# Count blocks built up to 42 quads ahead of the messages, two batches of visits a step behind them, and smaller layer 0 units from block 28 on

## Chip, cores and metric

One NeuronCore of a Trainium2 chip. The metric is the device time of one execution in microseconds (us); the median of the runs is compared.

## What is computed

Two graph layers on the same graph of 6,250 nodes and 200,000 edges, sorted by destination, features of width 128 in float32:

```
layer 0:  m   = silu([x[src], x[dst], edge_attr] @ W1 + b1) @ W2 + b2
          agg = segment_sum(m, dst)
          x1  = LN(x + LN(x + mlp([x, agg])) )
layer 1:  agg = segment_sum(x1[src], dst) / max(degree, 1)
          out = LN(x1 + relu(relu([x1, agg] @ W1 + b1) @ W2 + b2))
```

Layer 1 needs x1 of every source node, so it can start only where layer 0 has finished a block of nodes.

## The kernel before, in words

Edges come in tiles of 128, four tiles are a quad, seven quads a group: 391 quads with edges (NQ), 392 in all (QUADS), 56 groups. Nodes come in 49 blocks of 128 (NB). The main loop has a step for every quad. All five engines run the same loop over steps s (functions `fast` of `sync`, `gpsimd`, `vector`, `tensor`, `scalar` in build_edges), each with its own instruction order, joined by semaphores that count.

**The messages.** GpSimd gathers the rows P_d[src] of a quad with four indirect DMAs (line 885), up to seven quads ahead: the gather of quad s waits until VectorE has added quad s - 7. TensorE makes `products` (lines 1169 and 1172), VectorE adds the gathered rows (`add`, line 961), ScalarE applies silu (line 1384), TensorE sums the messages into the nodes of the group (`sums`, lines 1206 and 1208). After the seventh quad VectorE adds the group's sums to the sums of all nodes (`add_sums`, line 969).

**The counts.** For layer 1 the kernel makes, per group, a 128 x 6272 matrix of how often each source node meets each destination of the group. For every quad VectorE writes one-hot tiles (`hots`, lines 946 and 948) from the keys (`make_keys`, once a group, lines 913 to 922), TensorE multiplies them (`count`, line 1186, with a carry at line 1192), ScalarE copies the result into the buffer `counts` (`copy_counts`, line 1328, and a carry at line 1333). There are two such buffers, one for even and one for odd groups. When a group is complete, ScalarE's queue stores its buffer to HBM in four parts (`store`, line 1354), one a step at steps 1 to 4 of the next group; at step 5 VectorE waits for the four parts and zeroes the buffer for the group after that (`clear`, line 929). In the kernel before, the count of a quad is made in the step before its messages.

**Layer 0 units.** When all sums of a stretch of nodes are final, a unit of four blocks (UB) runs the update MLP and both layer norms in small parts over nine steps (`unit_step`) and leaves x1 in two float16 halves (x1h). The blocks 46 to 48 can only come after the last quad, as a unit that starts at step 392.

**Visits.** A visit (d, lo, hi) applies the count matrix of group d to the blocks lo to hi of x1: the matrix comes back from HBM (`load_visits`, line 774, on SyncE's queue), TensorE does two matmuls a block (`visit`, line 1222), VectorE adds the 128 x 120 result to the sums of layer 1 (`add_visit`, line 978). Each such addition begins with a register load of the group's base column. `plan_visits` puts them by hand: one batch of at most 14 blocks (VB) a step, at most two visits in it before step 392 and four from there on; a visit may come only when the blocks are ready and the matrix is stored.

**The end.** After step 391 come the last unit (steps 392 to 401), the remaining visits (to step 430) and, as visits complete, 13 last units of layer 1 (`last_step`: matmuls at lines 1282 to 1294, VectorE at 1087 to 1103, ScalarE at 1433 to 1445, then the store of the output), put into the steps by `plan_last`.

Of the kernel before, what the change touches and what calls it, by code (L numbers as in the profile page):

```python
# [24 lines left out]
P = 128  # L25
# [25 lines left out]
UB, LAST_B = 4, 46  # L51
# [3 lines left out]
RL, RZ = 8, 3  # L55
NQ = -(-(-(-N_EDGES // P)) // QT)
# [15 lines left out]
def plan_units():  # L72

    units, lo = [], 0
    while lo < LAST_B:
        hi = min(lo + UB, LAST_B)
        units.append((lo, hi, -(-(P * hi + SLACK) // 112) * GQ + 1))
        lo = hi
    return units + [(LAST_B, NB, QUADS)]


def plan_visits(units):

    done, visits, s = [0] * GROUPS, [], 0
    while sum(done) < GROUPS * NB:
        ready = max([hi for lo, hi, s0 in units if s0 + U_LEN <= s], default=0)
        zeroed = max([hi for lo, hi, s0 in units if s0 + 1 <= s], default=0)
        left = VB
        for _ in range(2 if s < QUADS else 4):
            best = None  # L90
            for d in range(GROUPS):
                if s < (d + 1) * GQ + GQ + 2 or zeroed < NB and 112 * d + SLACK + GW > P * zeroed:
                    continue
                n = min(ready - done[d], left)
                if n >= (4 if s < QUADS - 2 * GQ else 1) and (best is None or n > best[0] and (ready < NB or n > 9)):
                    best = (n, d)
            if best:
                n, d = best
                visits.append((s, d, done[d], done[d] + n))
                done[d] += n  # L100
                left -= n
        s += 1
# [8 lines left out]
VISITS_AT = {s: [i for i, v in enumerate(VISITS) if v[0] == s] for s, d, lo, hi in VISITS}  # L111
UNIT_AT = {s0 + k: (u, k) for u, (lo, hi, s0) in enumerate(UNITS) for k in range(-4, U_LEN + 1)}
LAST_VISIT = [max(i for i, (s, d, b0, b1) in enumerate(VISITS) if 112 * d - SLACK < P * hi) for lo, hi in LAST_UNITS]
# [3 lines left out]
def plan_last():  # L117

    start, now = {}, 0
    for s in range(QUADS, QUADS + 20 * GQ):  # L120
        start[s] = now
        blocks = sum(VISITS[i][3] - VISITS[i][2] for i in VISITS_AT.get(s, ()))
        now += max(0.1 * blocks, 0.3 * len(VISITS_AT.get(s, ())), 1.5 if s <= QUADS + U_LEN else 0.7)
    steps, first = [], 0
    for w in range(len(LAST_UNITS)):
        first = max(first, start[VISITS[LAST_VISIT[w]][0] + 1] + 2)
# [10 lines left out]
def plan_slots():  # L137
# [3 lines left out]
    for b, s in enumerate(sorted(VISITS_AT)):  # L141
        r = b % RA
        if s >= QUADS + LEAD:
            r, late = late % RT, late + 1
        slot[s], before[s], used[r] = r, used.get(r), s
        at, parts = 0, []
        for i in VISITS_AT[s]:
# [7 lines left out]
        pieces[s] = parts  # L155
        count[r] += len(parts)
        landed[s] = 16 * count[r]
# [6 lines left out]
def plan_loads():  # L164

    at, last = {}, 0
    for s in sorted(VISITS_AT):
        last = max(last, s - (AHEAD if s >= QUADS + AHEAD + LEAD else LEAD), -1 if BEFORE[s] is None else BEFORE[s])
        at.setdefault(last, []).append(s)
# [6 lines left out]
def plan_banks():  # L176

    bank, freed, last = [], [], [None, None]
    for k, s in enumerate(sorted(VISITS_AT)):
        for j, i in enumerate(VISITS_AT[s]):  # L180
            bank.append((k % 2, j))
            freed.append(last[k % 2])
        last[k % 2] = VISITS_AT[s][-1]
# [6 lines left out]
def changes_of_sums():  # L190

    n, at = 0, {}
    for s in range(ENDQ):
# [3 lines left out]
        for i in VISITS_AT.get(s - 1, ()):  # L197
            n += 1
            at["visit", i] = n
        if UNIT_AT.get(s, (0, 0))[1] == 1:  # L200
            n += 1
            at["zero", UNIT_AT[s][0]] = n
    return at
# [429 lines left out]
def build_edges(nc, ctx, sem, sb, v):  # L633
# [42 lines left out]
    first_i = [v["first_i0"], sb("first_i1", [P, GT], I32)]  # L676
    nodeE = [sb(f"nodeE{k}", [KQ, QT * P], BF16) for k in range(2)]
# [33 lines left out]
    onehots = sem("onehots")  # L711
    keyed, far, near = sem("keyed"), sem("far"), sem("near")
# [31 lines left out]
    def sync(sp):  # L744
# [17 lines left out]
        def load_visits(s):  # L762

            r = SLOT[s]
            if BEFORE[s] is not None:
                sp.wait_ge(l1_mm, VISITS_AT[BEFORE[s]][-1] + 1)
# [4 lines left out]
            for d, m, lo, hi, at in PIECES[s]:  # L771
# [48 lines left out]
        def fast():  # L820
            load_q(0)
            load_ids(1)
            v["table_stored"](sp)
            for s in range(ENDQ):
                g, q = divmod(s, GQ)
                if q == 1 and 1 <= g < GROUPS - 1:
                    sp.wait_ge(sum_mm, g * GQ)
                    load_ids(g + 1)
                unit_loads(s)
# [70 lines left out]
    def vector(dve):  # L900
        v["settled"](dve)
        V = nc.vector

        def make_keys(g):

            k = g % 2
            if g > 0:
                dve.wait_ge(s_in[k], 16 * ((g + 1) // 2))
            dve.wait_ge(i_in[k], 32 * (g // 2 + 1))
            D3 = dst_i[k][:]  # L910
# [1174 lines left out]
```

## Time and profile before

| | |
|---|---|
| median of 3 runs | 2164.84 us (2163.88 to 2165.56) |
| the profiled execution | 2164.69 us |
| its span, first to last instruction | 2162.5 us |
| busy: TensorE matmul / VectorE / ScalarE / GpSimd | 90% / 77% / 66% / 71% |
| mean granted clock of TensorE | 0.935 of full speed |
| indirect gathers of the loop | 1535 |
| additions of visits (line 978) | 432 |

The 2.2 us between span and time lie outside the instructions. Busy shares are means over the whole span and say little here: the start, the loop of 391 steps (from about 60 us to about 2015 us) and the end have different limits, and a queue that issues DMAs counts only the issue as busy.

### The profile page before, as it was taken

What the parts mean: (1) busy time and instruction counts of PE and PEld (TensorE: products, weight loads), DVE (VectorE), ACT (ScalarE), POOL (GpSimd) and SP (SyncE); (2) the same over time, 40 slices, a digit from 0 to 9 for tenths busy, and PEclk for the clock granted to TensorE, in tenths of its full rate; (3) what the DMA queues carried; (4) which work ended last, traced back from release to release, by engine and by line L of the source; (5) the groups of instructions that cost most, each with busy time, mean ns of one, the idle gap of its engine ahead of it and who ended that gap; (6) DMA issues with size and microseconds to landing.
All of it is one profiled execution on the core that took longest, in us unless ns stands there. A gap on an engine that the chain in (4) does not pass through costs nothing.

```text
span 2162.5 us, 59764 instructions
## 1 busy us (share of the span) xinstructions
PE 1943.1 (90%) x19625; PEld 1742.2 (81%) x19625; DVE 1669.0 (77%) x5633; ACT 1431.0 (66%) x3734; POOL 1530.5 (71%) x1633
## 2 busy tenths in 40 slices
PE   7898888888898898999998998998999999999885
PEld 7887777777787787888887887987888898998764
DVE  8688877877787887787887787888887878877344
ACT  3677766676686776776776676766776776776214
POOL 7577777777777777777777777777777777776121
PEclk9989988998898998998998999999999999999998
DMA  8567667675776776777787787888787798887871
GB/s 283 145 211 220 194 193 206 185 221 173 225 221 215 193 240 202 226 227 233 214 259 218 214 258 238 254 243 247 233 266 232 228 285 245 258 290 249 280 249 50
DMA packets 301154, 487.81 MB, mean 226 GB/s; under 512 B 120202, under 2 KB 175244, under 8 KB 300840
## 3 DMA queue, kind: packets, MB, share of 16 engines
q10 hardware_dynamic: 94017, 245.03, 34.4%
q1 hardware_dynamic: 154823, 129.94, 20.4%
q0 software_dynamic: 52000, 108.96, 19.3%
q8 instruction: 160, 2.62, 0.5%
q14 instruction: 154, 1.26, 0.2%
HBM read 375.62 MB, written 108.13 MB: 224 GB/s over the span
## 4 chain that ended last, share of the span: by engine, by line
POOL 48%; issue 19%; PE 15%; DVE 8%; DMA 7%; ACT 2%; DVEq 1%; ACTq 0%; SPq 0%; POOLq 0%
POOL gath L885 48%; DMA gath<-P_d,src_i 6%; PE ps_l L1222 3%; PE ps_pre L1169 3%; PE ps_cnt L1186 3%; DVE edgeK L948 2%; PE ps_sum L1206 2%; DVE pre L961 1%; DVE edgeL L946 1%; DVE sumT L978 1%; DVEq L975 1%; PE ps_p L435 1%; DMA A_v<-A_d 1%; PE ps_pre L1172 1%; ACT counts L1328 1%
## 5 line engine op out<-in xcount | busy, mean ns | idle before, releaser
L885 POOL DMA_INDIRECT gath<-P_d,src_i x1535 | 1455.3, 948 | 486.4 <-issue 455.4
L948 DVE TENSOR_SCALAR edgeK<-iotaK,key 128x500 bf16<-128x500 f16 (+1 forms) x1564 | 666.7, 486 | 0.0
L1169 PE MATMUL ps_pre<-wc,eT_c 128*128 128x128 f32 x3128 | 619.7, 320 | 2.4 <-issue 2.4
L1186 PE MATMUL ps_cnt<-edgeK,edgeL 128*128 128x250 bf16 (+1 forms) x3128 | 485.8, 304 | 78.9 <-ACT counts L1328 41.4
L1169 PEld LDWEIGHTS ps_pre<-wc,eT_c 128*128 128x128 f32 x3128 | 514.0, 206 | 25.3 <-issue 2.6
L1328 ACT ACTIVATE counts<-ps_cnt 128x1000 bf16<-128x1000 f32 x391 | 404.4, 1034 | 172.4 <-issue 90.5
L1206 PE MATMUL ps_sum<-edgeN,h 128*128 128x40 f32 x3128 | 428.1, 288 | 75.0 <-ACT h L1384 74.5
L1206 PEld LDWEIGHTS ps_sum<-edgeN,h 128*128 128x128 f32 x3128 | 398.3, 199 | 100.1 <-ACT h L1384 87.5
L961 DVE TENSOR_TENSOR pre<-ps_pre,gath 128x512 f32<-128x512 f32 x384 | 260.8, 679 | 266.7 <-DMA gath<-P_d,src_i 215.8
L1384 ACT ACTIVATE h<-pre 128x512 f32<-128x512 f32 x391 | 243.8, 624 | 264.3 <-DVE pre L961 262.7
L1186 PEld LDWEIGHTS ps_cnt<-edgeK,edgeL 128*128 128x128 bf16 x3128 | 290.9, 102 | 149.2 <-DVE edgeK L948 68.3
L1364 ACT ACTIVATE farN<-iotaN,rel_g 128x40 f32<-128x40 f16 x1564 | 381.1, 314 | 33.0 <-issue 31.0
L1172 PE MATMUL ps_pre<-Qw,nodeE 120*128 120x128 bf16 x1564 | 359.5, 230 | 0.0
L946 DVE TENSOR_SCALAR edgeL<-iotaL,low 128x132 bf16<-128x132 f16 x1564 | 327.2, 269 | 0.0
L1222 PE MATMUL ps_l<-A_v,x1h 128*128 128x120 bf16 x4856 | 295.3, 218 | 10.5 <-DMA A_v<-A_d 5.5
L1222 PEld LDWEIGHTS ps_l<-A_v,x1h 128*128 128x128 f16 x4856 | 271.9, 99 | 18.0 <-issue 8.1
L978 DVE TENSOR_TENSOR sumT<-ps_l,sumT 128x120 f32 x432 | 119.5, 277 | 101.0 <-PE ps_l L1222 47.5
L1172 PEld LDWEIGHTS ps_pre<-Qw,nodeE 120*128 120x128 bf16 x1564 | 164.4, 105 | 0.0
L1374 ACT ACTIVATE edgeN<-farN 128x160 f32<-128x160 f32 x391 | 125.9, 322 | 26.5 <-PE ps_sum L1208 26.2
L938 DVE TENSOR_SCALAR nodeE<-rel_c,pidq 120x512 bf16<-120x512 bf16 x391 | 141.2, 361 | 0.0
L1375 ACT ACTIVATE edgeB<-farN 128x160 bf16<-128x160 f32 x391 | 125.1, 320 | 0.0
L1333 ACT ACTIVATE carry<-counts 128x50 bf16 x335 | 96.6, 288 | 40.2 <-ACT counts L1328 0.8
(185 smaller groups left out, 1391.6 us busy)
## 6 DMA issues: line engine op xcount, KB each, us to landing
eT_c<-eT ACTq DMA_DIRECT2D x193, 512.0 KB
A_d<-counts ACTq DMA_DIRECT2D x168, 384.0 KB
rel_c<-rel_d ACTq DMA_DIRECT2D x193, 240.0 KB
A_v<-A_d SPq DMA_DIRECT2D x70, 448.0 KB
A_v<-A_d SPq DMA_DIRECT2D x111, 256.0 KB
gath<-P_d,src_i POOLq DMA_INDIRECT x1535
A_d<-counts ACTq DMA_DIRECT2D x56, 416.0 KB
Qw<-Q_d SPq DMA_DIRECT2D x56, 180.0 KB
```

Of the source, the lines that this page charges most:

```text
L885: pool.indirect_dma_start(gath[:, q, t * D:(t + 1) * D], None, v["P_d"], bass.IndirectOffsetOnAxis(ap=src_i[g % 2][:, c:c + 1], axis=0)).t ...
L946: V.tensor_scalar(edgeL[x][:, j, :], iotaL[:, :, 0:LC], low[k][:, q * QT + j:q * QT + j + 1], None, ALU.is_equal)
L948: last = V.tensor_scalar(edgeK[x][:, ROFF[j]:ROFF[j] + A2 * w], iotaK[j][:, :, 0:A2 * w // KR], key[k][:, q * QT + j:q * QT + j + 1], None ...
L961: V.tensor_tensor(pre[s % 2][:], ps_pre[s % 2][:], gath[:, q, :], ALU.add).then_inc(pre_add, 1)
L1169: T.matmul(o, eT_c[c % RE][:, e0:e0 + P], wc[:], start=True, stop=False)
L1172: last = T.matmul(o, nodeE[x][:, t * P:(t + 1) * P], Qw[g % 2][:, q, :], start=False, stop=True)
L1186: last = T.matmul(o[:, :, w0:w0 + w], edgeL[x][:, j, 0:P], r, start=(j == 0), stop=(j == QT - 1 and q == 0), skip_group_check=True)
L1206: T.matmul(ps_sum[:, cols], h[x][:, t, :], edgeN[x][:, t, :], start=False, stop=True, skip_group_check=True)
L1222: last = T.matmul(l1_part(i), x1h[:, a, part, :], A[:, (a - lo) * P:(a - lo) * P + GW], start=(a == lo and part == 0), stop=(a == hi - 1 a ...
L1328: A.activation(counts[k][:].rearrange("p (b a) d -> p b a d", b=2)[:, :, :, bass.ds(off, W0)], ps_cnt[:, :, 0:AB * W0].rearrange("p b (a d ...
L1364: last = A.activation(farN[:, j, :], iotaN[:, q, :, 0:WN // KR], ACT.Square, scale=-1.0, bias=rel_g[k][:, q * QT + j:q * QT + j + 1])
L1384: A.activation(h[x][:, :, 0:D], pre[x][:].rearrange("p (t n) -> p t n", n=D), ACT.Silu).then_inc(silu, 1)
```

## The change

- **Counts ahead.** `plan_counts` separates the step of a count from that of its quad. Until step 11 nothing changes. From step 12 to step 258, every sixth step makes a second ("extra") count, 42 in all, so that the counts run up to 43 quads ahead; the last count is made in step 347 instead of 390. Every extra count happens to be the seventh quad of a group. The stores of a group follow its copies, the clearing of a buffer follows the seventh one-hots of a group (now directly behind `hots`), and the keys of the next group are made behind its fourth.
- **Own index tiles.** The keys of group g + 1 are made from `src_c`, `dst_c`, `first_c`, loaded by three more small DMAs a group on SyncE's queue; the relative destinations of the messages are still made from the old tiles, in the new function `relate`.
- **Two batches a step.** Steps 357 to 391 have no count; they may have two batches of visits each, one ahead of `sums` and one behind, with up to three visits a batch. VectorE adds the first late in the same step and the second early in the next. `add_visits` reads all base columns of a batch before its first addition.
- **The ring of matrix buffers** grows from 4 to 12 slots at step 357 instead of 396, loads run 10 steps ahead from step 367 instead of 406.
- **Units of two blocks** from block 28 on: 17 units instead of 13.

What the planners give by this (blocks times groups, 2744 in all):

| | before | after |
|---|---|---|
| visits | 432 | 528 |
| block visits before step 392 | 2206 | 2392 |
| block visits from step 392 on | 538 | 352 |
| visits from step 392 on | 93 | 68 |
| of these in steps 392 to 404 | 15 | 12 |
| last step with a visit | 430 | 419 |
| last units with their VectorE part before the last visits | 8 | 3 |

The core of the diff:

```diff
-UB, LAST_B = 4, 46
+UB, LAST_B, FINE = 4, 46, 28
+EARLY, EVERY, FIRST_EXTRA = 42, 6, 12
...
-        hi = min(lo + UB, LAST_B)
+        hi = min(lo + (UB if lo < FINE else 2), LAST_B)
...
+def plan_counts():
+    main, extra, c, s = {}, {}, 1, 0
+    while c < NQ:
+        if s >= FIRST_EXTRA and s % EVERY == 0 and c - s - 1 < EARLY:
+            extra[s], c = c, c + 1
+        if c < NQ:
+            main[s], c = c, c + 1
+        s += 1
+    copied = {0: 0, **{c: s + 1 for s, c in main.items()}, **{c: s for s, c in extra.items()}}
+    stores = {}
+    for c in range(GQ, NQ):
+        if 1 <= c % GQ <= len(PARTS):
+            stores.setdefault(copied[c], []).append((c // GQ - 1, c % GQ - 1))
...
# plan_visits: t = 2 * step + (0 or 1)
+        s, second = divmod(t, 2)
+        if second and not COUNTED + LEAD <= s < QUADS:
+            t += 1
+            continue
-        for _ in range(2 if s < QUADS else 4):
+        for _ in range(2 if s < COUNTED + LEAD else 3 if s < QUADS else 4):
...
# vector
-        def add_visit(i):
-            base = dve.value_load(gbase[0:1, VISITS[i][1]:VISITS[i][1] + 1], min_val=0, max_val=NP_ - 1)
+        def add_visits(t):
+            made = VISITS_AT[t]
+            bases = [dve.value_load(gbase[0:1, VISITS[i][1]:VISITS[i][1] + 1], min_val=0, max_val=NP_ - 1) for i in made]
+            for i, base in zip(made, bases):
+                dve.wait_ge(l1_mm, made[-1] + 1)
+                dve.wait_ge(changed, CHANGE["visit", i] - 1)
+                V.tensor_tensor(sumT[:, bass.ds(base, GW)], l1_part(i), sumT[:, bass.ds(base, GW)],
+                                ALU.add).then_inc(changed, 1)
...
-                if s + 1 < NQ:
-                    if q == GQ - 1:
-                        dve.wait_ge(prepared, g + 2)
-                    hots(s + 1)
-                for i in VISITS_AT.get(s - 1, ()):
-                    add_visit(i)
+                for c in (COUNT_AT.get(s), EXTRA_AT.get(s + 1)):
+                    if c is not None:
+                        if c % GQ == 0:
+                            dve.wait_ge(prepared, c // GQ + 1)
+                        hots(c)
+                        if c % GQ == 3 and c // GQ + 1 < GROUPS:
+                            make_keys(c // GQ + 1)
+                        if c % GQ == GQ - 1:
+                            clear(c // GQ + 1)
+                for t in ADDED_EARLY.get(s, ()):
+                    add_visits(t)
                 unit_step(s)
                 split_biases(s)
                 if g + 1 < GROUPS and q == 2:
-                    make_keys(g + 1)
-                if g + 1 < GROUPS and q == 5:
-                    clear(g + 1)
+                    relate(g + 1)
...
+                if s in ADDED_LATE:
+                    add_visits(ADDED_LATE[s])
...
# tensor
-                for i in VISITS_AT.get(s, ()):
+                for i in VISITS_AT.get(2 * s, ()):
                     visit(i)
...
+                if s in EXTRA_AT:
+                    count(EXTRA_AT[s])
                 if s < NQ:
                     sums(s)
-                if s + 1 < NQ:
-                    count(s + 1)
+                for i in VISITS_AT.get(2 * s + 1, ()):
+                    visit(i)
+                if s in COUNT_AT:
+                    count(COUNT_AT[s])
...
# scalar
             for s in range(ENDQ):
+                made = 0 if s == 0 else COUNT_AT.get(s - 1)
+                if s + 1 < NQ:
+                    distances(s + 1)
+                if s in EXTRA_AT:
+                    copy_next(made)
                 if s < NQ:
                     activate(s)
                     load_chunk_of(s)
...
+                if s in EXTRA_AT:
+                    copy_next(EXTRA_AT[s])
+                elif made is not None:
+                    copy_next(made)
+                for g, part in STORES_AT.get(s, ()):
+                    store(g, part)
```

## Rows read from the trace of the kernel before

**Rows 1.** Page: chain that ended last, by engine; groups: line, op, xcount | busy, mean | idle.
```profile
POOL 48%; issue 19%; PE 15%; DVE 8%; DMA 7%; ACT 2%; DVEq 1%; ACTq 0%; SPq 0%; POOLq 0%
L885 POOL DMA_INDIRECT gath<-P_d,src_i x1535 | 1455.3, 948 | 486.4 <-issue 455.4
```

**Rows 2.** Line 885 and line 961, windows from 0 to 120 and 0 to 1300 us: count, min/median/max ns.
```profile
L885 POOL DMA_INDIRECT gath<-P_d,src_i x40: 938/944/1062, 69.4 to 119.9; - x40
L961 DVE TENSOR_TENSOR pre<-ps_pre,gath x5: 669/672/691, 102.4 to 117.1; 128x512 f32<-128x512 f32 x5
...
L885 POOL DMA_INDIRECT gath<-P_d,src_i x981: 938/944/1511, 69.4 to 1299.1; - x197
L961 DVE TENSOR_TENSOR pre<-ps_pre,gath x244: 619/690/693, 102.4 to 1297.7; 128x512 f32<-128x512 f32 x122
```

**Rows 3.** Busy time by stretch: PE, PEld, DVE, ACT, POOL, clock, DMA share, GB/s.
```profile
1920.00:1970.00 50.00, 50.00 (x634) 47.53 (x632) 40.84 (x147) 39.47 (x98) 37.81 (x41) 1.00 0.85 267
```

**Rows 4.** Timeline at the loop's end: start, duration, engine, line; in brackets idle before.
```profile
1993.03 0.94 POOL L885 DMA_INDIRECT gath<-P_d,src_i  x1 [0.30 <-issue]
...
2007.84 1.63 PE L1222 MATMUL ps_l<-A_v,x1h 128*128 128x120 bf16 x28
2009.31 1.04 PE L1206 MATMUL ps_sum<-edgeN,h 128*128 128x40 f32 x8
...
2008.04 0.69 DVE L961 TENSOR_TENSOR pre<-ps_pre,gath 128x512 f32<-128x512 f32 x1 [1.10 <-PE ps_pre L1172]
2014.74 0.29 DVE L969 TENSOR_TENSOR sumT<-ps_sum,sumT 128x128 f32 x1 [0.54 <-DVE sumT L978]
```

**Rows 5.** Waits of VectorE, windows 110:1370, then 900:1350: us, times, longest.
```profile
DVE pre L961 <- DMA gath<-P_d,src_i: 166.8, 75, 7.0
...
DVE pre L961 <- DMA gath<-P_d,src_i: 44.0, 22, 5.5
...
DVE counts L929 <- DMA A_d<-counts: 9.1, 4, 4.7
```

**Rows 6.** Timelines: VectorE's step and ScalarE's store; a store and the clearing it releases.
```profile
1136.81 0.68 DVE L961 TENSOR_TENSOR pre<-ps_pre,gath 128x512 f32<-128x512 f32 x1
1137.67 0.84 DVE L946 TENSOR_SCALAR edgeL<-iotaL,low 128x132 bf16<-128x132 f16 x4
1139.64 0.33 ACTq L1354 DMA_DIRECT2D A_d<-counts  x1
1140.05 0.27 DVE L978 TENSOR_TENSOR sumT<-ps_l,sumT 128x120 f32 x1
1141.51 0.69 DVE L961 TENSOR_TENSOR pre<-ps_pre,gath 128x512 f32<-128x512 f32 x1 [0.70 <-DMA gath<-P_d,src_i]
1145.87 0.33 ACTq L1354 DMA_DIRECT2D A_d<-counts  x1
...
1265.86 0.34 ACTq L1354 DMA_DIRECT2D A_d<-counts  x1
1270.77 0.72 DVE L929 MEMSET counts<- 128x800 uint32 x1 [1.81 <-DMA A_d<-counts]
```

**Rows 7.** Timeline of TensorE: the sums of a quad behind an idle stretch.
```profile
690.53 1.93 PE L1206 MATMUL ps_sum<-edgeN,h 128*128 128x40 f32 x8 [4.50 <-ACT h L1384]
```

**Rows 8.** Timelines of the end: a TensorE wait; VectorE's additions and last units.
```profile
2033.13 7.68 PE L1222 MATMUL ps_l<-A_v,x1h 128*128 128x120 bf16 x112 [4.60 <-DMA A_v<-A_d]
...
2051.79 0.28 DVE L978 TENSOR_TENSOR sumT<-ps_l,sumT 128x120 f32 x1 [2.87 <-PE ps_l L1222]
2052.61 0.28 DVE L978 TENSOR_TENSOR sumT<-ps_l,sumT 128x120 f32 x1 [0.54 <-PE ps_l L1222]
...
2135.80 0.68 DVE L1087 SCALAR_TENSOR_TENSOR eT_c<-ps_cnt,eT_c 128x512 f32<-128x512 f32 x1
2138.85 0.69 DVE L1087 SCALAR_TENSOR_TENSOR eT_c<-ps_cnt,eT_c 128x512 f32<-128x512 f32 x1 [0.79 <-PE ps_cnt L1294]
2142.63 0.69 DVE L1087 SCALAR_TENSOR_TENSOR eT_c<-ps_cnt,eT_c 128x512 f32<-128x512 f32 x1 [1.51 <-PE ps_cnt L1294]
```

More of the change, by code:

```diff
@@ L121, in plan_last @@
         start[s] = now
-        blocks = sum(VISITS[i][3] - VISITS[i][2] for i in VISITS_AT.get(s, ()))
-        now += max(0.1 * blocks, 0.3 * len(VISITS_AT.get(s, ())), 1.5 if s <= QUADS + U_LEN else 0.7)
+        blocks = sum(VISITS[i][3] - VISITS[i][2] for i in VISITS_AT.get(2 * s, ()))
+        now += max(0.1 * blocks, 0.3 * len(VISITS_AT.get(2 * s, ())), 1.5 if s <= QUADS + U_LEN else 0.7)
     steps, first = [], 0
     for w in range(len(LAST_UNITS)):
-        first = max(first, start[VISITS[LAST_VISIT[w]][0] + 1] + 2)
+        first = max(first, start[VISITS[LAST_VISIT[w]][0] // 2 + 1] + 2)
         steps += [(next(s for s in start if start[s] >= first + t), first + t, w, k) for k, t in enumerate(L_STEPS)]
@@ L140, in plan_slots @@
     count = [0] * RT
-    for b, s in enumerate(sorted(VISITS_AT)):
+    for b, t in enumerate(sorted(VISITS_AT)):
         r = b % RA
-        if s >= QUADS + LEAD:
+        if t // 2 >= COUNTED + LEAD:
             r, late = late % RT, late + 1
-        slot[s], before[s], used[r] = r, used.get(r), s
+        slot[t], before[t], used[r] = r, used.get(r), t
         at, parts = 0, []
-        for i in VISITS_AT[s]:
+        for i in VISITS_AT[t]:
             _, d, lo, hi = VISITS[i]
@@ L166, in plan_loads @@
     at, last = {}, 0
-    for s in sorted(VISITS_AT):
-        last = max(last, s - (AHEAD if s >= QUADS + AHEAD + LEAD else LEAD), -1 if BEFORE[s] is None else BEFORE[s])
-        at.setdefault(last, []).append(s)
+    for t in sorted(VISITS_AT):
+        s = t // 2
+        last = max(last, s - (AHEAD if s >= COUNTED + AHEAD + LEAD else LEAD), -1 if BEFORE[t] is None else BEFORE[t] // 2)
+        at.setdefault(last, []).append(t)
     return at
@@ L202, in changes_of_sums @@
             at["zero", UNIT_AT[s][0]] = n
+        for i in VISITS_AT[ADDED_LATE[s]] if s in ADDED_LATE else ():
+            n += 1
+            at["visit", i] = n
     return at
@@ L676, in build_edges @@
     first_i = [v["first_i0"], sb("first_i1", [P, GT], I32)]
+    src_c, dst_c, first_c = ([sb(f"{n}_c{k}", [P, GT], I32) for k in range(2)] for n in ("src", "dst", "first"))
     nodeE = [sb(f"nodeE{k}", [KQ, QT * P], BF16) for k in range(2)]
@@ L711, in build_edges @@
     onehots = sem("onehots")
+    related = sem("related")
+    c_in = [sem(f"c_in{k}") for k in range(2)]
     keyed, far, near = sem("keyed"), sem("far"), sem("near")
@@ L828, in fast @@
                     load_ids(g + 1)
+                for c in range(GQ + 1, NQ, GQ):
+                    if COUNT_STEP[c] == s and c // GQ + 1 < GROUPS:
+                        load_count_ids(c // GQ + 1)
                 unit_loads(s)
@@ L1106, in fast @@
         def fast():
+            relate(0)
             make_keys(0)
@@ L1451, in fast, with copy_next @@
         def fast():
-            off = 0
+            offset = [0]
+            def copy_next(c):
+                ahead = 0
+                if c % GQ < GQ - 1 and c + 1 < NQ:
+                    ahead = act.value_load(offs[0:1, c + 1:c + 2], min_val=0, max_val=LASTQ)
+                copy_counts(c, offset[0], ahead)
+                offset[0] = ahead
             distances(0)
```

100 lines of the change are left out of this document (53 added, 47 removed).

## The prediction, made before the kernel was run

> **What bounds the kernel now.** I read the page's chain first, then the groups of instructions, the stretches, and timelines of one step and of the end. In the chain GpSimd has 48% and nearly all of it is line 885 [rows 1]; the gathers take 0.948 us and are followed by 0.30 us of their own issue (455.4 us in 1494 gaps), so one comes every 1.25 us and a quad every 4.98 us. The reader is to see that GpSimd waits for nobody: 1535 gathers at that pace are 1915 us, and they run from 69.4 [rows 2] to 1993.03 [rows 4]. The loop cannot be shorter than that whatever the other engines do. Counting gathers / 4 less additions gives how far GpSimd leads VectorE beyond the seven quads of the start: 5.0 quads at 120 us, 1.25 at 1300 us [rows 2]. It may lead by 7. So 5.75 quads, 28.6 us, of lateness can be absorbed before a gather is held up.
>
> Late in the loop this changes: from 1920 to 1970 us TensorE is busy for 50.00 of 50 us at full clock [rows 3], because every step there has a full batch of 14 blocks, and the last gathers wait to be used. The quad of the last gather (1993.03) is added at 2008.04, and the last sums are in at 2014.74 [rows 4]. From there to the end of the span (2162.5) are 147.8 us. That tail is in three stretches. (1) 2014.74 to 2051.79: the last unit and 15 visits, with a wait of 4.60 us for a matrix. (2) 2051.79 to 2135.80: 78 visits, whose additions come 0.82 us apart in a chain on VectorE (0.28 us, then 0.54 us idle), with VectorE's part of 8 last units among them [rows 8]. 78 x 0.82 = 64, so the 8 units take the other 20, 2.5 us each. (3) 2135.80, the ninth last unit, to the end: 26.7 us; consecutive units are 3.78 us apart (2138.85, 2142.63) [rows 8].
>
> **The change, part by part.**
>
> *The counts leave the end of the loop.* After step 347 a step has no one-hots (2.38 us of VectorE: from 1137.67 to 1140.05 [rows 6]), no count on TensorE and no copy on ScalarE. TensorE is then no longer full at the end, and the addition of quad 390 follows its gather. The gather lands when VectorE could first use it: with the least lead seen, about 1 quad or 4 to 5 us behind the issue at 1993.03, at 1998.7. Then addition 0.69, silu and sums (1.04 us for their first part [rows 4]) need about 2.8 us: last sums at 2001.5 instead of 2014.74, if no gather was held up. Against it stand the six additions a step of steps 362 to 372 and 378 to 388. At 0.82 us each they are 4.9 us, more than the room; with the base columns read first, and under other work, 0.48 us each, 2.9 us, beside about 0.9 us for the rest. The bounds of a step are thus 3.8 and 5.8 us against 4.98, for some 22 steps: no lateness, or 18 us. I take 2 us.
>
> *The extra counts.* 42 of them, every sixth step (29.9 us of gathers). Each adds 2.38 us to VectorE. More: all are seventh quads, so `clear` now comes directly behind their one-hots, and the fourth part of the store it waits for is issued in the same step instead of the one before. From the addition the store is issued 2.83 us later (1136.81, 1139.64) or 4.36 (1141.51, 1145.87), and it takes 4.91 us to land (1265.86, 1270.77). VectorE reaches `clear` 3.24 us (1136.81 to 1140.05) plus 2.38 us behind the addition [rows 6]. So it waits between 2.1 and 3.65 us each time; I take 3.0. Queued behind it are this step's additions of visits and the next quad's addition, for which ScalarE and TensorE wait. Together 5.4 us per six steps. Against that stands the idle time which VectorE had: for gathers 166.8 us from 110 to 1370, of which 44.0 from 900 to 1350, and 9.1 us there for the same clearings [rows 5]. Per six steps that is 2.9 + 0.6 = 3.5 us late, and early (166.8 - 44.0) / 790 x 29.9 = 4.6 plus 0.7 for the lead won back, 5.3. Early the account is even. Late, 15 periods (steps 168 to 258, where most visits are) are short by 1.9 us each, 29 us: just the 28.6 us of lead. TensorE idles in each long step and then runs slowly: the sums behind 4.50 us of idle took 1.93 us [rows 7] against 1.04 [rows 4], which is the lower of the clock's two levels, 1.2 instead of 2.4 GHz. With the count as much again, at most 1.8 us each time, 27 us over 15 periods if all of it lay on the path and none if it lies beside VectorE's work; I take 8 us of held gathers.
>
> The Trainium skill ("DMA: Bandwidth & Descriptors", section on the anatomy of one DMA) has a fit for one DMA issued from GpSimd, 2.0 us plus the bytes at 436 GB/s. For a part of 384 KB that would be an estimate of 2.9 us where the trace shows 4.91 for a store from ScalarE's queue; the wait would then be 0.1 to 1.6 us instead of 2.1 to 3.65, and no gather would be held. The trace has the duration for the very transfer, so the sum goes by 4.91.
>
> *The tail.* Stretch 1: three visits and one batch of step 392 go (1.47 us on TensorE, 2007.84 to 2009.31 [rows 4], and 3 x 0.82 on VectorE), as does the matrix wait of 4.60, since loads now run ten steps ahead; with smaller waits behind it 11 us, 37 to 26. Bounds: 5 us (the unit's own chain of small steps sets it) and 13. Stretch 2: 56 visits instead of 78, 46 us, and 3 units at 2.6 among them instead of 8: 54 instead of 84. TensorE's 174 fewer blocks of this stretch (0.105 us each) lie beside this. Stretch 3: five more units at 3.78 before the last four: 26.7 + 18.9 = 46 us. Sum 126 instead of 147.8.
>
> *Costs beside other work.* Four more units between steps 246 and 380, in a stretch where ScalarE is busy for 39.47 of 50 us and VectorE for 40.84 [rows 3]; without that cover each would cost about what stretch 1 of the end takes without its visits, 37.1 - 15 x 1.47 = 15 us. Three more index DMAs a group stand on SyncE's queue, asked for two steps before their keys; if the queue were stuck behind a matrix load for more than two steps, the keys and all behind them would wait. `relate` moves one small subtraction. I cost them at nothing.
>
> *Sum.* 2001.5 + 8 + 2 = 2011.5, plus 126 is a span of 2137.5; with the 2.2 us around the span 2139.7. The profiled execution was 2164.69, the median 2164.84, so no correction: 2140 us, 1.1% less.
>
> **The rivals.**
>
> *The clearings don't bite.* VectorE's idle time takes them in and no gather is held: 2001.5 + 126 + 2.2, about 2130, or 2122 with the better bounds of the tail. For it: the waits for gathers are 166.8 us. Against it: they are not where the visits are.
>
> *The extra counts hold the gathers (slower).* Place: steps 12 to 258, VectorE in `clear`, GpSimd at line 885 for the addition of seven quads before. With 3.65 us of waiting and 1.8 us of cold clock each period costs 7.8 us: short by 2.5 in 27 periods and 4.3 in 15, 132 less 28.6 of lead, 103 us; 2001.5 + 103 + 126 + 2.2 = 2233. It decides against the change from a shortage of about 60 us, that is from 6.0 us a period on in place of 5.4 and something. Mild forms end between 2165 and 2190.
>
> *The late additions or the unit chain take back the gain.* Six additions a step at 0.82 give 16 us more than assumed, or the last unit's chain gives only 5 of 11: together 2160; one of them 2146 to 2156.
>
> *The change makes the counts early but the tail is not set by visits:* the 13 last units at 3.78 us are 49 us by themselves; were they to start no earlier than now, the tail would lose only stretch 1: 2150.
>
> **How the numbers follow.** My forecast has 0.42, clearings that don't bite 0.20, held gathers 0.20 (slower, nearly all), late additions or chain 0.12, unmoved tail 0.06. Two in a thousand of this kernel (4.3 us) is about what a measurement can tell from no change. Faster: all but the held gathers and a part of the late additions, 0.76; within 0.2%: 0.05; slower: 0.19. The range goes from 2122 (nothing held, best tail) to 2172 (the mild part of the slower case); the dear end of that case stays outside.
>
> **What the profile would show.** Gathers / 4 less additions at 1300 us: between 5 and 7 quads (forecast), under 3 (clearings don't bite), 7 from 600 us on, and waits of line 885 for line 961 (slower). Waits at line 929 of 2 to 4 us in about 42 places, some 120 us in all. Last gather near 2001, last sums near 2011, visits over 80 us behind that, and 56 additions in the last 54 of these. Wrong it would be above all if the gathers end after 2030, or if the clearings wait for under 1 us.

## The result and the profile after

The changed kernel takes 2361.93 us (median of 4 runs, 2356.34 to 2365.39) against 2164.61 for the kernel before: a ratio of 1.0913, 95% interval 1.0899 to 1.0926, or 197 us slower. The forecast was 2140 and 1.1% faster. The profiled execution has a span of 2358.9 us, 196.4 more than before, and everything below is told against spans. Four kernels were first run on a chip where the granted clock was 0.80 to 0.82, the kernel before took 2964.11 us, before_first 2982.91, extra_third 3055.43, both_units4 3057.73 and both_two 3057.86, and were run again elsewhere; only the later runs (labels ending in _b) are used, so nothing below is shown for such a chip.

The page of the kernel after, chain and groups (columns as in [rows 1]):

```profile
PE 38%; DVE 32%; issue 16%; DVEq 6%; ACT 5%; DMA 2%; ACTq 1%; SPq 0%; POOL 0%; POOLq 0%
...
L937 POOL DMA_INDIRECT gath<-P_d,src_i x1535 | 1455.6, 948 | 659.3 <-issue 440.4
L985 DVE MEMSET counts<- 128x800 uint32 (+1 forms) x56 | 42.6, 761 | 236.0 <-DMA A_d<-counts 235.7
```

GpSimd had 48% of the chain [rows 1] and has none of it now. The gathers are as many and as long as before, but the idle time ahead of them grew from 486.4 to 659.3 us. The second row is new among the costly groups: clearing a count buffer is 42.6 us of work with 236.0 us of idle VectorE ahead of it. The list of waits (engine, line, what it waited for: us, times, longest) says what was behind both:

```profile
DVE counts L985 <- DMA A_d<-counts: 235.7, 54, 8.2
POOL gath L937 <- DVE pre L1017: 99.7, 62, 12.3
POOL gath L937 <- DMA src_i<-src_pt: 99.2, 24, 10.9
```

In the kernel before, the same list had (line 929 is its clearing, line 961 its addition of gathers):

```profile
DVE pre L961 <- DMA gath<-P_d,src_i: 215.8, 110, 7.0
DVE counts L929 <- DMA A_d<-counts: 37.5, 18, 5.1
```

The waits for arriving gathers, which were VectorE's idle time before, are gone altogether. GpSimd now waits for VectorE (its lead of seven quads is used up), and at the turn of a group also for its own index tile, which SyncE loads only in the group before.

One clearing in full, from the timeline of the kernel after (answers to [rows 6] and [rows 7]):

```profile
993.22 0.69 DVE L1017 TENSOR_TENSOR pre<-ps_pre,gath 128x512 f32<-128x512 f32 x1 [0.96 <-PE ps_pre L1236]
994.84 1.71 DVE L1004 TENSOR_SCALAR edgeK<-iotaK,key 128x500 bf16<-128x500 f16 x4
998.57 1.71 DVE L1004 TENSOR_SCALAR edgeK<-iotaK,key 128x500 bf16<-128x500 f16 x4
999.75 0.33 ACTq L1422 DMA_DIRECT2D A_d<-counts  x1
1005.28 0.72 DVE L985 MEMSET counts<- 128x800 uint32 x1 [5.00 <-DMA A_d<-counts]
1008.65 0.66 DVE L1017 TENSOR_TENSOR pre<-ps_pre,gath 128x512 f32<-128x512 f32 x1
1009.34 0.63 ACT L1450 ACTIVATE h<-pre 128x512 f32<-128x512 f32 x1 [5.29 <-DVE pre L1017]
1009.58 0.94 POOL L937 DMA_INDIRECT gath<-P_d,src_i  x1 [8.29 <-DVE pre L1017]
1012.01 2.10 PE L1250 MATMUL ps_cnt<-edgeK,edgeL 128*128 128x250 bf16 x8 [0.80 <-DVE edgeK L1004]
```

VectorE writes the one-hots of two quads (line 1004 twice), is at the clearing at 1000.28 and stands there for 5.00 us, because ScalarE issued the fourth part of the store only at 999.75 and it landed 5.53 us later. The next quad's addition comes 15.4 us behind the one before it. ScalarE waited 5.29 us for it and GpSimd 8.29. The next count took TensorE 2.10 us. The Trainium skill ("PSUM — Partial Sum Buffer", section on engine and sequencer instructions) says that the queues of ScalarE, VectorE and GpSimd are strictly first in, first out; the trace agrees: the addition that GpSimd needed stood behind a clearing with which it has nothing to do.

Busy time by stretch in the kernel after (columns as in [rows 3]):

```profile
400.00:900.00 500.00, 429.72 (x3815) 377.08 (x3814) 392.01 (x1340) 335.26 (x865) 342.65 (x361) 0.88 0.66 197
900.00:1370.00 470.00, 399.30 (x3859) 354.19 (x3858) 359.63 (x1229) 302.46 (x777) 314.32 (x332) 0.90 0.69 206
1820.00:2100.00 280.00, 255.50 (x2921) 237.19 (x2921) 174.52 (x574) 165.57 (x456) 202.76 (x215) 0.94 0.86 259
```

No engine is full in any of them: VectorE is busy for 77 to 78% of the first two stretches and nevertheless sets the pace. Of the 108.0 and 110.4 us in which it is idle there, 71.7 and 71.1 are the wait at line 985. The granted clock of TensorE is 0.88 to 0.90 there.

The end of the loop and the end of the kernel (timelines; they answer to [rows 4] and [rows 8]):

```profile
2166.52 0.94 POOL L937 DMA_INDIRECT gath<-P_d,src_i  x1 [0.30 <-issue]
2208.80 0.29 DVE L1025 TENSOR_TENSOR sumT<-ps_sum,sumT 128x128 f32 x1 [2.55 <-PE ps_sum L1272]
...
2242.59 0.28 DVE L1036 TENSOR_TENSOR sumT<-ps_l,sumT 128x120 f32 x1 [0.21 <-DVE sumT L1036]
...
2243.55 0.28 DVE L1036 TENSOR_TENSOR sumT<-ps_l,sumT 128x120 f32 x1 [0.20 <-DVE sumT L1036]
2246.24 0.28 DVE L1036 TENSOR_TENSOR sumT<-ps_l,sumT 128x120 f32 x1 [2.40 <-PE ps_l L1286]
```

The 196.4 us lie in three places. The last gather is at 2166.52 instead of 1993.03 (173.5). The last sums follow it by 42.3 us instead of 21.7 (20.6). From there to the end of the span are 150.1 us instead of 147.8 (2.3). In the tail four additions come 0.48 us apart (0.28 and 0.20 idle), then 2.41 us of nothing: 2.2 us more than between two additions, so about 0.55 for each of the four reads of base columns. A batch of four takes 4.14 us (2242.10 to 2246.24), where single reads gave 4 x 0.82 = 3.28 [rows 8].

### The profile page after: what moved, and what is told of

It is laid out like the page before. It is cut to its first block, busy times and chain, and to the rows that moved or that the text cites. A ratio compares the mean times of both kernels' runs of the same rounds, so it can differ in the third digit from the quotient of the medians.

```text
span 2358.9 us, 60784 instructions
## 1 busy us (share of the span) xinstructions
PE 2020.4 (86%) x19657; PEld 1803.8 (76%) x19657; DVE 1706.5 (72%) x5757; ACT 1457.9 (62%) x3770; POOL 1530.9 (65%) x1633
## 4 chain that ended last, share of the span: by engine, by line
PE 38%; DVE 32%; issue 16%; DVEq 6%; ACT 5%; DMA 2%; ACTq 1%; SPq 0%; POOL 0%; POOLq 0%
DVE edgeK L1004 13%; PE ps_pre L1233 9%; PE ps_cnt L1250 9%; PE ps_l L1286 7%; PE ps_sum L1270 6%; DVE edgeL L1002 6%; DVEq L1032 4%; DVE pre L1017 3%; DVE sumT L1036 3%; DVE nodeE L994 2%; PE ps_pre L1236 2%; ACT counts L1396 2%; DMA first_i<-dst_first 1%; ACT h L1450 1%; DMA A_v<-A_d 1%
## 5 line engine op out<-in xcount | busy, mean ns | idle before, releaser
L937 POOL DMA_INDIRECT gath<-P_d,src_i x1535 | 1455.6, 948 | 659.3 <-issue 440.4
L1233 PE MATMUL ps_pre<-wc,eT_c 128*128 128x128 f32 x3128 | 627.8, 323 | 2.6 <-issue 2.6
L1250 PE MATMUL ps_cnt<-edgeK,edgeL 128*128 128x250 bf16 (+1 forms) x3128 | 501.1, 310 | 64.1 <-ACT counts L1396 40.7
L1233 PEld LDWEIGHTS ps_pre<-wc,eT_c 128*128 128x128 f32 x3128 | 523.6, 210 | 28.9 <-issue 2.7
L1270 PE MATMUL ps_sum<-edgeN,h 128*128 128x40 f32 x3128 | 442.9, 294 | 100.0 <-ACT h L1450 99.4
L1270 PEld LDWEIGHTS ps_sum<-edgeN,h 128*128 128x128 f32 x3128 | 412.0, 205 | 120.6 <-ACT h L1450 108.2
L1250 PEld LDWEIGHTS ps_cnt<-edgeK,edgeL 128*128 128x128 bf16 x3128 | 299.1, 104 | 143.1 <-issue 43.6
L1286 PE MATMUL ps_l<-A_v,x1h 128*128 128x120 bf16 x4320 | 275.0, 222 | 82.4 <-DVE sumT L1036 80.0
L1286 PEld LDWEIGHTS ps_l<-A_v,x1h 128*128 128x128 f16 x4320 | 250.6, 101 | 92.5 <-issue 86.4
L1036 DVE TENSOR_TENSOR sumT<-ps_l,sumT 128x120 f32 x528 | 147.6, 280 | 227.5 <-PE ps_l L1286 116.1
L985 DVE MEMSET counts<- 128x800 uint32 (+1 forms) x56 | 42.6, 761 | 236.0 <-DMA A_d<-counts 235.7
```

The costliest lines, as they stand in the source:

```text
L937: pool.indirect_dma_start(gath[:, q, t * D:(t + 1) * D], None, v["P_d"], bass.IndirectOffsetOnAxis(ap=src_i[g % 2][:, c:c + 1], axis=0)).t ...
L1233: T.matmul(o, eT_c[c % RE][:, e0:e0 + P], wc[:], start=True, stop=False)
L1250: last = T.matmul(o[:, :, w0:w0 + w], edgeL[x][:, j, 0:P], r, start=(j == 0), stop=(j == QT - 1 and q == 0), skip_group_check=True)
L1270: T.matmul(ps_sum[:, cols], h[x][:, t, :], edgeN[x][:, t, :], start=False, stop=True, skip_group_check=True)
L1286: last = T.matmul(l1_part(i), x1h[:, a, part, :], A[:, (a - lo) * P:(a - lo) * P + GW], start=(a == lo and part == 0), stop=(a == hi - 1 a ...
```

## The experiments

My theory after reading this profile: two faults add up. The clearing now stands right behind the one-hots of a quad whose step also brings the last store (the greater part, in the loop), and the reads of all base columns ahead of a batch lengthen each batch by about 0.2 us an addition (at the loop's end and in the tail). The rivals: the 42 extra counts and the additional visits are themselves too much for VectorE; or the index tiles of the gathers, for which GpSimd waits 99.2 us, come too late by themselves.

### The clearing later, the bases singly, both, and no extra counts

**clear_later** puts the clearing behind the one-hots of the next group's first quad.

```diff
-                        if c % GQ == 0:
-                            dve.wait_ge(prepared, c // GQ + 1)
                         hots(c)
+                        if c % GQ == 0:
+                            clear(c // GQ)
...
-                        if c % GQ == GQ - 1:
-                            clear(c // GQ + 1)
```

> The changed kernel (2361.9 us) with the clearing of a count buffer moved one step later: behind the one-hots of the first quad of the next group, not of the seventh quad. Counts, visits and all costs stay. Theory A (the clearings hold VectorE, its lateness holds the gathers): the clearing waits fall from 235.7 us to under 90, the last gather comes before 2080 instead of 2166.5, the time is 2250 to 2290. Rival B (the extra one-hots and counts are too much by themselves, wherever the clearing stands): the clearing waits fall but the last gather stays beyond 2130 and the time beyond 2320. Rival C (the index tiles of the gathers come late, 99 us of waits at the gather line): these waits stay near 99 us and hold the time beyond 2300.

Measured: 2221.06 us (the kernel before took 2166.66 on that chip), span 2219.2. This and the next three kernels, and the four with _b, were executed once each; how far single executions of one kernel can lie apart is seen at both_again. Two waits from the list of waits:

```profile
DVE counts L985 <- DMA A_d<-counts: 44.1, 28, 4.1
POOL gath L937 <- DMA src_i<-src_pt: 30.8, 8, 7.4
```

The clearing's wait fell from 235.7 to 44.1 us and the time by 140.9 us, more than I had expected. The wait for the index tile fell with it, from 99.2 to 30.8, and is 6.6 in the kernel with both edits: it followed the lateness and was no cause of its own. All of the gain is in the loop: the last gather is at 2026.7 (139.8 us earlier), while the last sums still follow it by 42.4 us and the tail is still 150.1 us.

**base_each** reads each base column right before its own addition, as in the kernel before.

```diff
-            bases = [dve.value_load(gbase[0:1, VISITS[i][1]:VISITS[i][1] + 1], min_val=0, max_val=NP_ - 1) for i in made]
-            for i, base in zip(made, bases):
+            for i in made:
+                base = dve.value_load(gbase[0:1, VISITS[i][1]:VISITS[i][1] + 1], min_val=0, max_val=NP_ - 1)
```

> The changed kernel with each base column read right before its own addition of a visit, as in the kernel before, instead of all of a batch first. Theory (a read costs the sequencer some 0.55 us and is hidden under an addition only if it stands between two): a batch of four visits in the end takes 3.3 us instead of 4.14, the 15 batches there 12 us less, the steps with six visits about 1 us less each; the time is 2325 to 2345. Rival (reading first hides the reads, as I had forecast): 2362 to 2385.

Measured: 2319.31 us, 42.6 less than the changed kernel and a little beyond the range. The last gather comes 14.4 us earlier (2152.1), the last sums follow it by 25.6 us instead of 42.3, and the tail is 139.8 us instead of 150.1. The clearing still waits 241.4 us. Each edit moves mainly its own parts of the time: the lag of the last sums and the tail move with the reads, the waits of the clearing with its place.

**both** has both edits.

> Both edits together: clearing one step later, base columns read one by one. If the two causes are separate, the gains add: 2215 to 2270. If the lateness at the clearings only uncovers another limit (index tiles, late steps), less than the sum: beyond 2280.

Measured: 2165.32 us, 196.6 below the changed kernel and 50 below my range. That is 13 us more than the sum of the two alone (140.9 + 42.6 = 183.5), but this kernel scatters by more than that, as the rounds below show, so whether the two help each other stays open. The page and waits of this kernel:

```profile
PE 30%; DVE 21%; POOL 20%; issue 13%; ACT 6%; DMA 4%; DVEq 3%; ACTq 2%; SPq 0%; POOLq 0%
...
L937 POOL DMA_INDIRECT gath<-P_d,src_i x1535 | 1454.8, 948 | 491.7 <-issue 456.1
...
DVE pre L1017 <- DMA gath<-P_d,src_i: 46.8, 24, 7.4
DVE counts L985 <- DMA A_d<-counts: 42.1, 25, 4.2
```

The gathers run freely again, to 1998.0. VectorE has 46.8 us of waiting for gathers left of 215.8 in the kernel before. In rounds (**both_again**) this kernel took 2168.07 us (2157.42 to 2184.81), a ratio of 1.0015 with an interval of 0.9986 to 1.0044: level with the kernel before, and 193.9 us below the changed kernel. Its profiled execution, the third slowest of ten, has the last gather at 2004.8 and the last sums at 2034.7, where that of both has 1998.0 and 2023.7: differences of that size between single executions show nothing.

> The same kernel as in both, timed in rounds: 2162 to 2169 us, not to be told from the kernel before.

**no_extra** keeps everything of the change but makes no count ahead (`EARLY` 0 instead of 42).

> The changed kernel without any extra count: each count in the step before its quad, so clearings stand as in the kernel before; own index tiles, the reading of base columns first and units of two blocks stay; the planner then leaves 456 block visits and 77 visits for step 392 on and no step has two batches. Theory A: the last gather comes within 10 us of 1993 and the time is 2165 to 2195. Rival D (the new index tiles or the finer units hold the loop): the last gather comes after 2030 and the time is over 2210.

Measured: 2170.67 us. So 191 of the 197 us need the extra counts, though the clearing stands in the same place in both kernels: without them it waits 99.0 us in 39 places, and VectorE's idle time takes that in (waits for gathers: 124.4 us).

### Is it the extra counts or where they stand?

**extra_third_b** moves nothing but the phase of the extra counts. Since every extra count pushes the counts on by one quad, a count every sixth step always falls on the same quad of a group of seven. With the first at step 36 that is the third instead of the seventh.

```diff
-EARLY, EVERY, FIRST_EXTRA = 42, 6, 12
+EARLY, EVERY, FIRST_EXTRA = 42, 6, 36
```

> Only the place of the 42 extra counts moves: with the first at step 36 instead of 12 each of them is the third quad of its group, no longer the last one, behind whose one-hots the next group's count block is cleared. The last store of the group before leaves with a group's fifth quad, so that between it and the clearing there are two steps again instead of one. Theory A (the extra count eats the step that the store needs to land): the waits in front of the clearing fall from 236 us to 40 to 70 us and the time from 2362 to 2205 to 2250 us, as with the clearing moved behind the next quad (2221 us). Rival B (a count block more in any step makes VectorE late, wherever it stands): the waits fall, but others take their place, 2300 to 2365 us.

Measured: 2243.15 us (before on that chip: 2162.99), 119 us less than the changed kernel by one constant, and in the range of theory A:

```profile
DVE counts L985 <- DMA A_d<-counts: 96.3, 44, 5.9
POOL gath L937 <- DMA src_i<-src_pt: 60.0, 16, 9.7
DVE pre L1017 <- DMA gath<-P_d,src_i: 16.3, 6, 4.4
```

The waits at the clearing are those of no_extra (96.3 beside 99.0), with all 42 extra counts made. The difference to 235.7 is the place of the extra counts alone. They are above the 40 to 70 us I expected, and some 60 us above the 37.5 of the kernel before. That `clear` now stands ahead of the visits can account for about 0.8 us at each of 54 clearings, 43 us in all (VectorE is there 3.4 us behind its addition on average, in the kernel before 4.2); no run moves this alone.

**before_first_b** is the kernel before with its base columns read ahead of each batch.

> The kernel before, with nothing changed but that the base columns of a batch's visits are read one behind the other, ahead of its additions. Theory A (a read costs VectorE about 0.5 us unless an addition runs beside it): 482 visits in some 240 batches leave one read less covered for each visit but the first of a batch, about 240 x 0.5 = 120 us of VectorE's time, of which the slack takes most: 2170 to 2215 us. Rival B (the reads cost only where VectorE is the bound anyway, at the end): 2163 to 2172 us.

Measured: 2171.87 us against 2162.99, in both ranges, which overlap; the profile speaks for rival B. (For the first run of this kernel I had expected 2178 to 2190.) The loop does not suffer (last gather 1992.6, last sums 2009.2, even 5.6 us earlier than before), the tail does: 160.5 us instead of 147.8. Its timeline there:

```profile
2052.71 0.28 DVE L979 TENSOR_TENSOR sumT<-ps_l,sumT 128x120 f32 x1 [1.78 <-PE ps_l L1222]
...
2053.68 0.28 DVE L979 TENSOR_TENSOR sumT<-ps_l,sumT 128x120 f32 x1 [0.20 <-DVE sumT L979]
2056.38 0.28 DVE L979 TENSOR_TENSOR sumT<-ps_l,sumT 128x120 f32 x1 [2.41 <-PE ps_l L1222]
```

The profile puts the 2.41 us down to TensorE, but the same gap before a batch of four stands in the changed kernel, and base_each closes it with TensorE's work unchanged: there the additions of the tail come 0.82 us apart within a batch and from one batch to the next. The reads are what is last.

### What is left between 2165 and the forecast

Both edits give 2165.3, not 2140. The loop of that kernel ends at 2023.69, 25.7 us behind the last gather. Its VectorE in one of the late steps (timeline):

```profile
2004.41 0.68 DVE L1017 TENSOR_TENSOR pre<-ps_pre,gath 128x512 f32<-128x512 f32 x1
2005.27 0.27 DVE L1036 TENSOR_TENSOR sumT<-ps_l,sumT 128x120 f32 x1
2006.03 0.28 DVE L1036 TENSOR_TENSOR sumT<-ps_l,sumT 128x120 f32 x1 [0.48 <-DVE sumT L1036]
2006.85 0.28 DVE L1036 TENSOR_TENSOR sumT<-ps_l,sumT 128x120 f32 x1 [0.54 <-DVE sumT L1036]
...
2009.51 0.68 DVE L1017 TENSOR_TENSOR pre<-ps_pre,gath 128x512 f32<-128x512 f32 x1
```

Six additions of visits make this step 5.10 us, which is short for its kind: the 20 steps with six take 5.60 on average (5.09 to 7.16), slower than a quad of gathers (4.98). In the changed kernel, with the reads first, the same 20 steps take 6.63 (5.88 to 8.09).

**both_two_b** (at most two visits in a late batch instead of three) and **both_units4_b** (units of four blocks throughout, `FINE` 46) each add one edit to both.

> Clearing moved and base columns read singly (2165.3 us), and on top at most two visits in a batch of the late steps instead of three. Theory A (the steps of six additions set the end of the loop, 26 us behind the last gather): with four additions in a step it follows the last gather by 12 to 20 us, 2152 to 2163 us, less what more visits behind the loop cost. Rival B (the end waits for the last sums through TensorE's own queue): 2163 to 2172 us.

> Clearing moved and base columns read singly (2165.3 us), and on top the units of layer 0 are of four blocks throughout, as in the kernel before (503 visits instead of 528). Theory A (the four more units and 25 more visits cost VectorE and ScalarE in the late part what they bring behind the loop): 2158 to 2170 us. Rival B (units of two blocks shorten the tail by bringing the visits earlier): 2172 to 2190 us.

Measured: 2158.21 and 2158.88 us (before on that chip: 2162.99), both in the ranges of theories A; but executions of both alone reach from 2157.42 to 2184.81, so neither time decides. The profiles say more. With two visits a batch the last sums follow the last gather by 13.2 us instead of 25.7 (29.9 in both_again), and the 24 steps with four additions take 4.78 on average. With units of four blocks the lag is 22.3 us and the tail 139.2 instead of 139.8: the finer units bring the tail nothing. Whether they cost the loop anything is not shown.

**both_units4_two** has the four edits, **four_no_extra** the same without extra counts, **four_third** the same with the extra counts on third quads.

> Clearing moved, base columns read singly, units of four blocks throughout and at most two visits in a late batch: the four edits together. On their own the last two brought 6.4 us (units) and 7.1 us (two visits) on top of 2165.3 us. Theory A (they take weight off the same late steps, one each): 2148 to 2156 us, the last sums 12 to 18 us behind the last gather. Rival B (both only bring the loop's end up to the last gather, which stays): 2156 to 2160 us.

> The four edits, and no count block made ahead: 432 visits, of which 538 blocks in 93 visits lie behind step 392, instead of 368 blocks in 76 visits. Theory A (the extra counts buy what the visits behind the loop cost, some 17 visits and 170 products with TensorE): 8 to 18 us slower than the four edits with them, 2160 to 2172 us. Rival B (the early counts and visits cost the loop what they save behind it): within 4 us of it.

> The four edits, and the first extra count at step 36, so that the extra counts are third quads. Theory A (with the clearing behind the next quad's one-hots the store has time in either place, so the place of the extra counts no longer matters): within 5 us of the four edits, clearing waits 20 to 60 us. Rival B (a last quad counted early still hurts): faster than them by 5 to 15 us.

| kernel (three rounds) | us | ratio to before (2164.63) | interval |
|---|---|---|---|
| both_units4_two | 2155.47 | 0.9951 | 0.9933 to 0.9968 |
| four_no_extra | 2161.45 | 0.9981 | 0.9971 to 0.9991 |
| four_third | 2153.32 | 0.9940 | 0.9922 to 0.9958 |

The extra counts are worth 6.0 us (2161.45 less 2155.47), or 8.1 in their other place; under the 8 to 18 I expected, above the 4 of the rival. Between the two places the intervals overlap, as theory A has it; but the clearings of four_third wait for no store at all, where I had expected 20 to 60 us. Where four_third gains and gives back, by its profile and that of four_no_extra: last gather 1998.4 and 1992.7, last sums 2010.8 and 2009.2, tail 141.5 and 150.4 us. Its VectorE still waits for gathers:

```profile
L1017 DVE TENSOR_TENSOR pre<-ps_pre,gath 128x512 f32<-128x512 f32 x384 | 261.5, 681 | 172.1 <-DMA gath<-P_d,src_i 106.4
```

That is 106.4 us against 235.1 in four_no_extra. The 42 extra counts put 42 x 2.38 = 100 us more of VectorE's work into the loop up to step 282 (it is gone again from the late steps), and the last gather moved by 5.7 us only: the idle time did take the work in. four_third, in the end four edits and one constant away from the changed kernel, is 0.6% faster than the kernel before and the fastest here.

The tail has no such slack. In both it runs in three stretches: 2023.69 to 2055.25 (the last unit and the first visits, 31.6 us), to the last unit at 2108.39 (53.1), and this to the end (timeline of line 1145, one row for each last unit of layer 1):

```profile
2108.39 0.68 DVE L1145 SCALAR_TENSOR_TENSOR eT_c<-ps_cnt,h 128x512 f32<-128x512 f32 x1
2113.28 0.69 DVE L1145 SCALAR_TENSOR_TENSOR eT_c<-ps_cnt,h 128x512 f32<-128x512 f32 x1 [1.00 <-PE ps_cnt L1356]
2121.74 0.68 DVE L1145 SCALAR_TENSOR_TENSOR eT_c<-ps_cnt,hT_u 128x512 f32<-128x512 f32 x1
2127.29 0.69 DVE L1145 SCALAR_TENSOR_TENSOR eT_c<-ps_cnt,z_u 128x512 f32<-128x512 f32 x1 [2.57 <-PE ps_cnt L1356]
2132.25 0.69 DVE L1145 SCALAR_TENSOR_TENSOR eT_c<-ps_cnt,xT_u 128x512 f32<-128x512 f32 x1 [2.69 <-PE ps_cnt L1356]
2136.03 0.69 DVE L1145 SCALAR_TENSOR_TENSOR eT_c<-ps_cnt,eT_c 128x512 f32<-128x512 f32 x1 [1.51 <-PE ps_cnt L1356]
```

The visits are done at 2108; ten last units remain, and the first four gaps are 4.89, 8.46, 5.55 and 4.96 us before the pace of 3.78 is reached. In the kernel before, most of these units lay among the visits. What fills the second gap is in the timeline of both (line 1161 is a small VectorE instruction of the last units, line 946 GpSimd's multiplication of the sums by 1/degree, one for each last unit):

```profile
2115.38 6.44 DVE L1161 SCALAR_TENSOR_TENSOR shift_l<-mv_l,rs_l 128x4 f32<-128x4 f32 x1
2115.65 6.55 POOL L946 TENSOR_TENSOR sumT<-sumT,deg 128x512 f32<-128x512 f32 x6
```

The instruction usually takes 0.16 us. With the last visits done, GpSimd makes its last six multiplications in one run, and VectorE's instruction ends only when the fifth, the last of full width, is over. That is 6.3 of the 8.7 us by which the first four gaps exceed that pace. No run moved these multiplications, so it is seen and not tested.

## Why the prediction was wrong, by its steps

- **The gathers, 1.25 us each, and the lead that absorbs lateness: right, with a gap.** Same instructions, same mean, and in both and four_third they end at 1998. But 5.75 quads of absorbable lateness was too many near the turn of a group: GpSimd waits 99.2 us for an index tile that is loaded only in the group before, once the sums of the group before that are made (in the kernel before: 1.6 us), which I had not looked at.
- **The extra counts, the step that failed.** I took 3.0 us for the wait at the clearing, from bounds of 2.1 to 3.65, in 42 places. Between 110 and 1430 us it was 191.3 us in 40 places, 4.8 each (2.25 to 7.44), outside the bounds. The means of the three terms over these 40 places, read from the timelines: the fourth part is issued 4.93 us behind the addition (3.70 to 6.97), where I had 2.83 to 4.36 from two ordinary steps; the store lands 5.76 us behind its issue (3.7 to 8.4), where I had the 4.91 of one store; and VectorE is at `clear` 5.91 us behind the addition instead of 5.62. 4.93 + 5.76 - 5.91 = 4.8. In the example above it is 6.53 + 5.53 - 7.06 = 5.0; there ScalarE's silu began 4.08 us behind the addition, behind two table loads of 1.28 us. ScalarE copies one count between the silu and the store, as before: what was mis-sized is a wait taken from one landing and two issues. The trace of the kernel before had better values: the 18 clearings that waited there stood until 3.2 to 9.6 us behind the issue, 5.66 on average, and ScalarE's stores between 110 and 1430 us left 4.16 us behind the addition of their step; 4.16 + 5.66 - 5.62 would have given 4.2.

  The other 12 clearings, which I costed at nothing, wait 29.5 us in all.
- **Idle time against it.** The account per six steps was right for the work: 100 us of one-hots cost the gathers 5.7 us. It was wrong for the wait. Moving the clearing took away 191.6 us of waiting and 139.8 us of lateness at the last gather; nearly three parts in four of the wait went through. These runs do not show that waiting costs more than work of the same length: in the changed kernel VectorE had no wait for gathers left that could take it in, in four_third it had 106.4 us. Whether the colder clock had a share of its own was not tried; the mean clock was 0.901, and 0.948 in both.
- **Base columns read first, the second failure, and one of sign.** I counted 0.48 us an addition "with the base columns read first", seeing only the gap between additions and not the reads ahead of them. The batch of four costs 1.04 us an addition, more than the 0.82 of before. The 42.6 us that base_each gave are 14.4 in the loop, 16.7 from the last gather to the last sums and 10.3 in the tail, together 41.4 of span. The bounds of a late step were 3.8 and 5.8 us; with single reads it took 5.60 on average, within them, in the changed kernel 6.63, outside.
- **Counts leave the loop's end: right as a mechanism, eaten by the visits.** I had 2011.5 for the last sums; the kernel with both edits reached 2023.7 with six additions a step, four_third 2010.8 with four.
- **The tail, 126 us: too hopeful by 14 even with the bases mended.** In both it is 139.8. Stretch 1 was 31.6 where I had 26 (bounds of 5 and 13 us saved: it saved 5.5, near the bound at which the last unit's own chain sets it), stretch 2 53.1 against 54, and stretch 3 55.1 against 46: five more units at 3.78 were right, but the first four gaps cost 8.7 us more than that pace, 6.3 of them in the one stretched VectorE instruction.
- **The store's duration.** The Trainium skill ("DMA: Bandwidth & Descriptors", section on the anatomy of one DMA) gives by its fit, which is for a DMA issued from GpSimd, an estimate of 2.9 us for a part of 384 KB. The trace had 4.91 and after the change 5.53 in the example and 5.76 on average, so the measurement decides again, as in the forecast.
- **The rival that held the gathers** was the right mechanism at the right place: clearings, VectorE late, GpSimd waiting. I gave it 0.20 and 2233 us because its dear end used the same upper bound of 3.65 us. With 4.8 in its place the rival's own sum gives 2281 us, an estimate (42 x 1.15 more), and with the 41.4 us of the reads 2323; the rest of the 2362 is not separated, but the tail's 14 us and the 29.5 us at the other clearings are of its size. The signs named in advance read so: waits at line 985 above the 2 to 4 us, waits of the gathers for the addition present, lead between 4.5 and 7 quads from 600 to 1500 us, gathers ending after 2030.

## What to carry to other kernels

When a step is moved, list what its release now stands behind on the other engines' queues: here a clearing that waits for a store, in the very step in which ScalarE issues that store behind its silu and a copy. Take the length of such a wait from all the stores of a trace and not from one or two. A wait in an in-order queue ahead of work that another engine needs costs little while the queue has idle time to give, and most of its length when it has none (here nearly three parts in four). And a regular insertion (every sixth step in groups of seven) can hit the same worst place each time, so shift its phase before judging the idea. Reads that set up an instruction pay when they alternate with the instructions, and cost when they are gathered ahead of them.

## What the runs showed that was not expected

- A register read of a base column costs VectorE about 0.54 us and is partly hidden beside an addition: 0.82 us for a read and an addition in turn, 1.04 for four reads and then four additions (4.14 us).
- One 128 x 4 instruction of the last units (`shift_l`, line 1161, usually 0.16 us) is stretched beside GpSimd's multiplications of 128 x 512 (line 946, 1.25 to 1.28 us each). Beside one of them it took 1.80 us at the longest; beside five in a row 5.77 us in the kernel after, 6.44 in both and 5.72 in four_third. Each time it ended 0.02 to 0.03 us behind the end of such a multiplication. In the kernels without extra counts GpSimd makes no such row of six, and there the longest is 1.80. The additions of visits beside the same multiplications kept their 0.28 us. Why it is stretched was not tried.
- The kernel with both edits scatters by 27 us between executions (2157.42 to 2184.81), the kernel before by 6 us (2162.23 to 2168.34).
